# Decoder layer with tree cross-attention: the weighted V rows summed four at a time by a reduction over a strided axis

## What is computed

```python
# K, V: heads of ctx; flatK, flatV: the tree's 1023 nodes (leaves first)
nk, nv = flatK[:, :, idx_table], flatV[:, :, idx_table]      # 12 nodes per token, same table for all sequences
self_logits = einsum('bhnd,bhnd->bhn', Q, K) * scale
nbr_logits = einsum('bhld,bhlnd->bhln', Q, nk) * scale
w = softmax(concatenate([self_logits[..., None], nbr_logits], -1))
out = einsum('bhln,bhlnd->bhld', w, concatenate([V[:, :, :, None], nv], 3)) @ Wo.T + bo
```

## Time and profile before

| | us |
|---|---|
| median of 3 runs (lowest, highest) | 2518.28 (2516.43, 2519.88) |
| profiled execution: its own time | 2520.97 |
| its span, first to last instruction | 2519.1 |
| busy over the span: PE, DVE, POOL, ACT | 2154.1, 1723.4, 1062.2, 774.9 |
| DMA queue of the gathers: packets, MB | 55296, 201.35 |

### The profile page before, as it was taken

The page is one execution under the profiler, slowest core; times in us unless marked ns, Lnnn a source line. Parts: engine busy times, 40 slices in busy tenths (PEclk is TensorE's granted clock), DMA queues, the critical chain, the costliest instruction groups (busy, mean ns, idle before and its releaser), DMA issues.

```text
span 2519.1 us, 30969 instructions
## 1 busy us (share of the span) xinstructions
PE 2154.1 (86%) x9824; PEld 1027.8 (41%) x9824; DVE 1723.4 (68%) x2321; ACT 774.9 (31%) x1143; POOL 1062.2 (42%) x1108
## 2 busy tenths in 40 slices
PE   5899999999999999972388888888898888988997
PEld 2333333333333333320145455444454454544554
DVE  7555647464747566536788787878888788787850
ACT  3344444444445444540012121221122121221212
POOL 3233324232324142324354645555465555556431
PEclk9999999999999999995689999999999999999999
DMA  6333424142434323219655646465564646556420
GB/s 206 109 117 101 133 84 134 63 127 92 135 93 133 102 94 109 94 66 326 234 166 197 207 160 221 145 226 179 180 211 164 228 156 208 185 184 206 159 76 22
DMA packets 175789, 379.72 MB, mean 151 GB/s; under 512 B 19748, under 2 KB 69028, under 8 KB 175656
## 3 DMA queue, kind: packets, MB, share of 16 engines
q0 software_dynamic: 55296, 201.35, 22.9%
q1 hardware_dynamic: 120360, 176.85, 22.0%
HBM read 306.57 MB, written 71.30 MB: 150 GB/s over the span
## 4 chain that ended last, share of the span: by engine, by line
DVE 23%; issue 15%; DMA 8%; PE 3%; POOL 3%; DVEq 0%; ACT 0%; POOLq 0%; SPq 0%
DMA nb<-kv_flat,idx_rows 8%; DVE logits L1279 5%; DVE o_sb L1342 4%; DVE nb L1329 4%; POOL nb L1460 3%; PE bank L1096 2%; DVE nb L1270 2%; DVE nb L1337 1%; PE bank L1084 1%; DVE stats L1371 1%; DVE x L1369 1%; DVE own L1274 1%; DVE logits L1283 1%; DVE stats L1390 1%; DVE top L1301 1%
## 5 line engine op out<-in xcount | busy, mean ns | idle before, releaser
L690 DVE TENSOR_REDUCE neg_max<-rows_ps 128x2 f32<-128x1024 f32 x256 | 312.4, 1220 | 314.9 <-PE rows_ps L485 314.0
L1096 PE MATMUL bank<-w_sb,hid 128*128 128x512 f32 x1024 | 505.2, 617 | 0.9 <-ACT hid L1208 0.9
L1460 POOL DMA_INDIRECT nb<-kv_flat,idx_rows x384 | 392.1, 1021 | 184.3 <-issue 99.9
L1270 DVE TENSOR_TENSOR nb<-nb,bank 128x1024 f32<-128x1024 f32 x192 | 231.2, 1219 | 210.2 <-DMA nb<-kv_flat,idx_rows 169.8
L1208 ACT ACTIVATE hid<-bank,b_sb 128x256 f32<-128x256 f32 x256 | 120.5, 471 | 742.9 <-PE bank L1084 654.1
L610 ACT ACTIVATE probsT<-e_ps 128x1024 f32<-128x1024 f32 x256 | 261.9, 1023 | 168.4 <-PE e_ps L513 167.9
L1084 PE MATMUL bank<-x2T_hi,w_hi_sb 128*128 128x256 f16 x1024 | 280.7, 274 | 10.1 <-DVE x2T_lo L1379 10.0
L1084 PE MATMUL bank<-x2T_lo,w_hi_sb 128*128 128x256 f16 x1024 | 280.3, 274 | 0.0
L1084 PE MATMUL bank<-x2T_hi,w_lo_sb 128*128 128x256 f16 x1024 | 280.2, 274 | 0.0
L503 PE MATMUL o_ps<-probsT,v_sb 128*33 128x512 f32 x1024 | 272.9, 612 | 6.3 <-ACT oT L607 6.1
L1488 POOL TENSOR_TENSOR nb<-nb,weights 128x1024 f32<-128x1024 f32 x96 | 195.2, 2061 | 156.4 <-DVE weights L1316 156.4
(11 more groups left out here) (123 smaller groups left out, 2960.1 us busy)
## 6 DMA issues: line engine op xcount, KB each, us to landing
kv_flat<-kv_nat SPq DMA_DIRECT2D x128, 256.0 KB, 2.6
own<-kv_flat SPq DMA_DIRECT2D x32, 512.0 KB
q_stack<-qk_dram SPq DMA_DIRECT2D x96, 128.0 KB, 2.7
k_stack<-qk_dram SPq DMA_DIRECT2D x96, 128.0 KB, 3.0
in_sb<-in_xT SPq DMA_DIRECT2D x8, 1024.0 KB, 6.5
in_sb<-in_ctxT SPq DMA_DIRECT2D x8, 1024.0 KB, 6.7
qk_dram<-hi SPq DMA_DIRECT2D x32, 256.0 KB, 2.2
qk_dram<-lo SPq DMA_DIRECT2D x32, 256.0 KB, 2.7
```

The source lines that it names most:

```text
L690: dve.tensor_reduce(neg_max[:, g % 2, at:at + 2], rows_ps[:], AX.X, ALU.max, negate=True).then_inc(max_done, 1)
L1096: mm = pe.matmul(ACC[i][:], hid[:, c % 2, i * P:(i + 1) * P], w2_sb[:, c, :], start=False, stop=c == WC - 1)
L1270: dve.tensor_tensor(kk, kk, q.unsqueeze(1).to_broadcast([P, GN, D]), ALU.mult)\
L1460: pool.indirect_dma_start(nb[:, slot(lt, g), k, :], None, kv_flat, bass.IndirectOffsetOnAxis(idx_rows[:, lt, at:at + 1], 0))\
```

## The change

The two steps `pair` and `accumulate` for each of 6 groups become `reduce` and `accumulate` for each of 3 pairs of groups. One `tensor_reduce` takes the 4 weighted V rows of two adjacent slots, seen as 512 columns of 4 elements each, and writes their sums to a new buffer `part_sum`. In memory the 4 elements of a column lie 4 KB apart, the next column 4 bytes on. Gathers now wait on the semaphore that this reduction counts up (`v_sum`), no longer on `accumulate`, and both slots of a pair come free with it. The order in `values` is written out anew, and POOL weights its last group (5) only after it has issued the first group of gathers. The small bias buffers of the start now lie inside the `x2` and `x2T` buffers, and `part_sum` is new.

```diff
+SUMS = NG // 2
...
+            part_sum = sb("part_sum", [P, SUMS, D])
...
-                    pe.wait_ge(o_part, START + (b * TT + lt + 1) * (NG + 1))
+                    pe.wait_ge(o_part, START + (b * TT + lt + 1) * (SUMS + 1))
...
-                    def pair(g):
...
-                        v = nb[:, slot(lt, g), :, D:2 * D]
-                        dve.tensor_tensor(v[:, 0, :], v[:, 0, :], v[:, 1, :], ALU.add).then_inc(v_pair, 1)
-                    def accumulate(g):
-                        dve.wait_ge(v_pair, START + n * NG + g + 1)
-                        dve.wait_ge(o_part, START + n * (NG + 1) + g + 1)
-                        dve.tensor_tensor(o, o, nb[:, slot(lt, g), 0, D:2 * D], ALU.add).then_inc(o_part, 1)
+                    def reduce(k):
+                        g = 2 * k + 1
+                        dve.wait_ge(v_mul_dve, START + n * len(DVE_V_GROUPS) + sum(d <= g for d in DVE_V_GROUPS))
+                        dve.wait_ge(v_mul_pool, START + n * len(POOL_V_GROUPS) + sum(d <= g for d in POOL_V_GROUPS))
+                        first = slot(lt, 2 * k)
+                        dve.tensor_reduce(part_sum[:, k, :], nb[:, first:first + 2, :, D:2 * D]
+                                          .rearrange("p s n d -> p d (s n)"), AX.X, ALU.add).then_inc(v_sum, 1)
+                    def accumulate(k):
+                        dve.wait_ge(v_sum, START + n * SUMS + k + 1)
+                        dve.wait_ge(o_part, START + n * (SUMS + 1) + k + 1)
+                        dve.tensor_tensor(o, o, part_sum[:, k, :], ALU.add).then_inc(o_part, 1)
                     multiply(0)
...
-                    for g in range(NG):
-                        if g + 1 in DVE_V_GROUPS:
-                            multiply(g + 1)
-                        pair(g)
-                        if g:
-                            accumulate(g - 1)
-                        if g == 0:
-                            between()
-                    accumulate(NG - 1)
+                    multiply(1)
+                    reduce(0)
+                    between()
+                    multiply(2)
+                    accumulate(0)
+                    reduce(1)
+                    accumulate(1)
+                    reduce(2)
+                    accumulate(2)
...
-                        pool.wait_ge(o_part, START + summed(b, i - SLOTS))
+                        pool.wait_ge(v_sum, START + summed(b, i - SLOTS))
...
-                    return b * (TT * (NG + 1)) + i // NG * (NG + 1) + i % NG + 2
+                    return b * (TT * SUMS) + i // NG * SUMS + i % NG // 2 + 1
...
-                        weight_values(b, lt)
+                        weight_values(b, lt, POOL_V_GROUPS[:-1])
...
-                        for i in range((lt + 1) * NG + AHEAD, (lt + 2) * NG + AHEAD):
+                        for k, i in enumerate(range((lt + 1) * NG + AHEAD, (lt + 2) * NG + AHEAD)):
                             if more or i < TT * NG:
                                 gather(b, i)
+                            if k == 0:
+                                weight_values(b, lt, POOL_V_GROUPS[-1:])
```

More of the change, by code:

```diff
@@ L845, in decoder_layer @@
             b1_sb = sb("b1_sb", [P, WC])
-            bias_in = sb("bias_in", [2, 2, D])
-            bias_hi = sb("bias_hi", [2, 2, D], F16)
-            bias_lo = sb("bias_lo", [2, 2, D], F16)
             bias_rows = sb("bias_rows", [2, 2, D], F16)
@@ L870, in decoder_layer @@
             x2T_lo = sb("x2T_lo", [P, KC, T], F16)
+            bias_in, bias_hi, bias_lo = x2[0:2, 0:2, :], x2T_hi[0:2, 0:2, :], x2T_lo[0:2, 0:2, :]
             hid = sb("hid", [P, 2, RW])
@@ L888, in decoder_layer @@
             norm_step, weights_ready = sem("norm_step"), sem("weights_ready")
-            v_mul_dve, v_mul_pool, v_pair, o_part = sem("v_mul_dve"), sem("v_mul_pool"), sem("v_pair"), sem("o_part")
+            v_mul_dve, v_mul_pool, v_sum, o_part = sem("v_mul_dve"), sem("v_mul_pool"), sem("v_sum"), sem("o_part")
             x1_loaded = [sem("x1_loaded0"), sem("x1_loaded1")]
@@ L964, in load_own @@
                     if not (isinstance(b, int) and b == 0 and lt == 0):
-                        sp.wait_ge(o_part, START + (b * TT + lt - 1) * (NG + 1) + 1)
+                        sp.wait_ge(o_part, START + (b * TT + lt - 1) * (SUMS + 1) + 1)
                         stand_alone(sp)
@@ L1158, in _ @@
                 act.wait_ge(consts2, START + CONSTS2)
-                act.activation(bias_hi[:], bias_in[:], ACT.Copy).then_inc(bias_step, 1)
+                act.activation(bias_hi, bias_in, ACT.Copy).then_inc(bias_step, 1)
                 def turned(b, lt, kind):
@@ L1427, in _ @@
                 dve.wait_ge(bias_step, START + 2)
-                dve.tensor_tensor(bias_lo[:], bias_in[:], bias_hi[:], ALU.subtract).then_inc(bias_step, 1)
-                dve.tensor_scalar(bias_rows[:], bias_hi[:], ident[0:2, 0:1], None, ALU.mult).then_inc(bias_step, 1)
+                dve.tensor_tensor(bias_lo, bias_in, bias_hi, ALU.subtract).then_inc(bias_step, 1)
+                dve.tensor_scalar(bias_rows[:], bias_hi, ident[0:2, 0:1], None, ALU.mult).then_inc(bias_step, 1)
                 dve.wait_ge(bias_step, START + 4)
-                dve.scalar_tensor_tensor(out=bias_rows[:], in0=bias_lo[:], scalar=ident[0:2, 1:2], in1=bias_rows[:],
+                dve.scalar_tensor_tensor(out=bias_rows[:], in0=bias_lo, scalar=ident[0:2, 1:2], in1=bias_rows[:],
                                          op0=ALU.mult, op1=ALU.add).then_inc(bias_step, 1)
@@ L1480, in next_rows, with weight_values @@
                     pool.wait_ge(idx_ready, START + n + 3)
-                def weight_values(b, lt):
+                def weight_values(b, lt, groups):
                     pool.wait_ge(weights_ready, START + b * TT + lt + 1)
-                    for g in POOL_V_GROUPS:
+                    for g in groups:
                         pool.wait_ge(gathered[slot(lt, g)], (16 * GN) * fills(b, lt, g))
```

## The result

The changed kernel takes 2526.43 us, median of 7 runs, against 2518.28 for the kernel before: ratio 1.0032, 95% interval 1.0021 to 1.0044. It is slower, as forecast, but by 8 us and not by 18.

What follows compares the result with a forecast made beforehand. The bound was a loop of slot free, gather, keys, values, slot free. Even +0.45 and odd +0.8 average 0.6 us a tile, over 30 tiles +18, so a median of 2536 us against 2518.28; range 2478 to 2600.

Steps and rivals of the forecast that it cites:

- the collision: In odd tiles DVE's first accumulate waits beside POOL's third weighting until 12.2 us, taking some 2 us instead of 0.68.
- The price of a reduction: Each new DVE reduction: 4.0 us, near the measured stride's 3.61, with something for slow reads hidden in the fixed time.
- the likeliest case's own range: 2524 to 2555 us, for strided reductions of 3.6 to 4.4 us with the collision; chance 0.40.
- The even tile: Even tiles: first gather earlier, eighth 0.7 us later behind POOL's moved weighting; less drained DMA backlog, net +0.45 us.
- The odd tile: Odd tiles: eighth gather 1.5 us later, less 0.7 us of drained DMA backlog, net +0.8 us.
- The later eighth gather: Odd tiles: late second release moves POOL's eighth gather start from 19.84 to 21.4 us, +1.5.
- The wait for rows: Odd tiles before the last key product: rows land at about 28.2 us, DVE's own work is done at 27.5.
- No change: Rival for the whole kernel: the terms cancel within 5 us; chance 0.10.
- PE at nothing: PE gets o_sb 5 us and x2T_lo 2.4 us later; costed at nothing, as PE already idles 3.5 us a tile.
- Full-rate reads: Rival: reductions cost only 2.28 to 2.42 us, -1.9 us a tile, -57 in all, so 2461; chance 0.14.
- No collision: Rival: reductions at 3.6 us, odd accumulate not held by POOL's weighting, -0.7 us a tile, so 2497; chance 0.22.
- DVE as the bound: Rival: reductions at 4.98 us make DVE's own work set the pace, +82 us, so 2600; chance 0.14.

Runs made afterwards that it cites:

- e1: Changed kernel with each reduction over four neighbouring elements instead of rows 4 KB apart (wrong sums, same work): 2461.33 us, ratio 0.9749 to the kernel before.
- e2: Changed kernel with POOL's third weighting back ahead of the gathers: 2499.11 us, ratio 0.9903 to the kernel before.
- e3: Changed kernel with accumulate 0 put behind the second reduction: 2514.80 us, ratio 0.9964 to the kernel before.
- m1: Small separate kernel timing reduction forms alone: 2048 elements take 2286 ns contiguous, 3.62 us at a 4 KB stride.
- b1: Kernel before with DVE's loop over the sequences written out: 2508.51 us, ratio 0.9975 to the kernel before.
- e4: Changed kernel with each reduction replaced by one addition of 1024 contiguous columns and two accumulations of 512: 2492.07 us, ratio 0.9897 to the kernel before.
- e6: e5 with group 3 weighted by DVE instead of POOL: 2447.21 us, ratio 0.9720 to the kernel before.
- e7: e6 with DVE's loop over the sequences written out: 2421.76 us, ratio 0.9603 to the kernel before.
- e5: e4 with POOL's three weightings ahead of the gathers and all three additions ahead of the accumulations: 2499.32 us, ratio 0.9920 to the kernel before.

## Why the prediction was right in direction and wrong in size

**What bounds the kernel** was read correctly: a turn of slots, gathers, keys and values. The experiments move the time in the way that the working gives: by the reduction's length (e1), by the place of the third weighting (e2), by the collision (e3).

**The price of a reduction**, "I take 4.0", was 3.78; the measured stride alone gave 3.61, and alone on the engine it is 3.62. The allowance for a hidden part was wrong (m1); the 0.16 us that the kernel adds were not foreseen. No run shows a reduction of 4.4 us, the upper end behind the likeliest case's own range (2524 to 2555): the strided forms of 2048 elements took 3.57 to 3.78 us in m1, and 3.78 in the kernel.

**The even tile** was to be 0.45 us slower. Over the 26 tiles from the fifth to the thirtieth, even ones went from 39.09 to 39.43 us: 0.34.

**The odd tile**, "+0.8", is the term that failed: 40.94 became 40.86 in the two profiles. Three steps of it can be told apart.
- *The later eighth gather, "+1.5"*, was 0.7 (20.1 to 20.8). After the change it started 0.6 earlier than the 21.4 forecast: POOL's third weighting was over at 11.95 and not 12.2, the accumulate ended half a microsecond behind it, and the reduction took 3.8 and not 4.0. And the 19.84 of before was taken from one tile; the odd tiles with `lt` 3 started it at 20.2.
- *The wait for rows* was to end last, at 28.2, over DVE's own 27.5. The rows were there by 27.2, where DVE's own work ended, so the path through odd tiles was DVE and not the gathers. From the eighth gather to the last key product it took 6.5 us, against 7.3 before: at least 0.8 drained, where the forecast had 0.7.
- *What the kernel before lost at the end of DVE's loop* was in no term. Its idle time there goes with packets of the instruction queue, which the changed kernel, with 6 operations and fewer waits in place of 12, does not fetch: none from 1510 to 2380 us, and its tiles at the loop's end take 40.7 to 40.9 us, like most other odd ones. The kernel before without that loop is 6.4 us faster (b1).

Against that kernel the sum is nearly right: the ratio 1.0032 over 0.9975 is 1.0057, or +14.5 us, near the +18; less the 6.4 us of the loop, 8. That is 0.5 us a tile, where the sum has 0.6. (Its profile gives 0.71 us for even and 0.77 for odd tiles, part of which is the faster chip.) That the removal of the loop and the change save the same 6.4 us is inferred from the packets and the waits; the changed kernel was not run without its loop. How the missing 10 us divide between the loop and the smaller delay of the gathers stays open, since a difference of a few microseconds between executions is as large as either part.

The sign rested on the collision, and that was there. But the margin was thin: both errors made the change look dearer than it is, and 3 us less would have been the "No change" case.

**PE at nothing** held for the time, but not with much to spare: PE's waits for o_sb and x2T_lo grew by 75 us in all while those for x2 fell by 78 (98.9 to 21.3), which is the exchange that the prediction named. DVE waited 2.2 us in all for the query projection.

**The rivals.** Full-rate reads: refuted for this kernel; e1, which has them, comes to 2455 on the scale of the record, 6 us from the rival's 2461. No collision: refuted, 2.14 us. DVE as the bound: true for the odd tiles already at 3.78 us, but without the jump in time, since DVE's work ended at 27.2, before the 28.2 at which the forecast had the rows.

## What to carry to other kernels

Look at the stride of the innermost axis before one instruction replaces several: here one addition of 1024 contiguous columns and one more accumulation (1.22 + 0.60 us) do what a strided reduction of 2048 elements did in 3.78 (e4). When slots come free earlier, move nothing in front of the transfers that were to profit (putting the third weighting back ahead of them gave 1.2%, e2), and look for the DVE addition with both inputs in SBUF that now falls beside a GpSimd weighting (2.14 us for 0.69 here). And look at the row of the instruction queue: 81 packets in the kernels with a loop of more operations, 55 in those with the changed kernel's `values`. Together with idle time put down to issue at the same place of each pass (27.1 us in five passes of e6) it is worth a run with the loop written out, which brought those 27.1 us to 0.3 (e7).

## What was not expected of the hardware

- The reduction of 2048 f32 has a step between 8 and 16 bytes of stride: 1.05 ns an element contiguous and at 8 bytes, 1.68 to 1.78 at 16, 32 and 64 bytes and at 2 and 4 KB; 16 and 32 bytes (3.78 us) are slower than the other three (3.57 to 3.62) (m1).
- At the end of a pass of its loop DVE stood idle for up to 5.8 us with a packet of instructions under way in the same idle time, while the DMA engines moved 368 GB/s (e6, 1841 to 1846 us); writing the loop out took 1.2% off that kernel and 6.4 us off the kernel before. The changed kernel's loop, with fewer operations, fetched nothing in five passes (1510 to 2380 us).
- DVE additions with both inputs in SBUF took longer beside a GpSimd weighting: 2.14 us for 0.69, ending 0.55 us behind it (changed kernel), 2.05 for 1.22 and 2.86 for 1.42 (e4). GpSimd's small operations took longer beside such additions: an index operation 1.26 us (e5) for 0.60 (kernel before).
